# Gated cross-attention and a 64-expert layer on one core: token gathers held by landings instead of progress marks, and the last softmax sums moved ahead of the last values

## The reference

```python
x = x + tanh(g_xattn) * xattn(layernorm(x), ctx_512)     # x: (2, 256, 256)
x = x + tanh(g_ffn) * ffn(layernorm(x))

def xattn(q, latent_kv):                  # 16 heads of width 16, causal
    qp = q @ Wq.T
    k, v = split(latent_kv @ Wkv_expand.T)      # latent_kv: (2, 512, 64)
    attn = softmax(where(causal, qp_h @ k_h.T / 4, min))
    return (attn @ v) @ Wout.T

def ffn(x):                               # 512 tokens, 64 experts, the best 8 of each token
    topw, topi = top_k(softmax(x @ router_weight.T), 8); topw = topw / sum(topw)
    # each expert takes the first 128 of its tokens, in the tokens' order
    h = silu(xe @ gate) * (xe @ up)       # 256 -> 96 for each half
    ye = h @ down                         # 96 -> 256
    return sum over a token's 8 experts of topw * ye
```

## Time and profile before

| | |
|---|---|
| median of 3 runs | 226.35 us (223.43 to 227.15) |
| the profiled execution's own time | 225.09 us |
| its span, first to last instruction | 223.3 us |
| TensorE matmul busy | 209.1 us, 94% |
| VectorE busy | 140.0 us, 63% |
| ScalarE busy | 110.4 us, 49% |
| GpSimd busy | 105.5 us, 47% |
| granted TensorE clock | 1.00 of full speed, in all 40 slices |

### The profile page before, as it was taken

The page is one execution under the profiler, slowest core; times in us unless marked ns, Lnnn a source line. Parts: engine busy times, 40 slices in busy tenths (PEclk is TensorE's granted clock), DMA queues, the critical chain, the costliest instruction groups (busy, mean ns, idle before and its releaser), DMA issues.

```text
span 223.3 us, 5260 instructions
## 1 busy us (share of the span) xinstructions
PE 209.1 (94%) x1676; PEld 166.2 (74%) x1676; DVE 140.0 (63%) x443; ACT 110.4 (49%) x350; POOL 105.5 (47%) x145
## 2 busy tenths in 40 slices
PE   7889999999999779899999899998989999999983
PEld 3556767776557247688998798888879888999973
DVE  6366354476498976637666665656666656348765
ACT  2525445434634926555555564645665555444431
POOL 7301222222262457555655556575555754756630
PEclk9999999999999999999999999999999999999999
DMA  5699999999011234787898898988755655223222
GB/s 153 191 301 282 305 283 250 246 251 236 23 59 23 68 103 128 208 222 217 237 288 245 255 250 276 246 252 276 212 141 160 173 157 157 73 70 83 84 70 94
DMA packets 37725, 41.03 MB, mean 184 GB/s; under 512 B 3874, under 2 KB 35044, under 8 KB 37700
## 3 DMA queue, kind: packets, MB, share of 16 engines
q1 hardware_dynamic: 32932, 27.21, 43.8%
q0 software_dynamic: 4048, 12.98, 22.0%
q10 hardware_dynamic: 720, 0.52, 0.8%
HBM read 32.97 MB, written 7.74 MB: 182 GB/s over the span
## 4 chain that ended last, share of the span: by engine, by line
PE 69%; DVE 8%; DMA 8%; issue 6%; ACT 3%; POOL 2%; another core or an unknown queue 2%; ACTq 0%; DVEq 0%; POOLq 0%
PE bank L789 13%; PE scores L807 10%; PE bank L779 8%; PE scores L779 6%; PE scores L769 6%; PE bank L574 5%; PE bank L589 4%; PE bank L813 4%; DMA gate_w<-xn_dram,slot_token 3%; PE scores L555 3%; DMA gate_w<-in_ctx_dram 3%; PE bank L518 2%; PE bank L537 2%; DMA xe<-xn_dram,slot_token 2%
## 5 line engine op out<-in xcount | busy, mean ns | idle before, releaser
L497 POOL DMA_INDIRECT gate_w<-xn_dram,slot_token x56 | 57.7, 1031 | 40.4 <-issue 15.0
L789 PE MATMUL bank<-y_high,scatter 128*128 128x256 f32 x156 | 45.0, 315 | 0.1
L789 PE MATMUL bank<-y_low,scatter 128*128 128x256 f32 x156 | 39.7, 281 | 0.0
L1280 DVE TENSOR_SCALAR scatter<-tokens,slot_token 128x256 fp32r<-128x256 f32 (+1 forms) x64 | 24.9, 390 | 22.9 <-PE bank L789 19.2
L807 PE MATMUL scores<-down_all,work 96*128 96x256 f32 x128 | 38.2, 380 | 0.7 <-DVE y_low L1293 0.7
L1003 ACT ACTIVATE gate_w<-scores,gate_w 128x256 f32<-128x256 f32 x42 | 20.0, 475 | 27.9 <-PE scores L807 16.3
L428 POOL TENSOR_SCALAR_AFFINE_SELECT gate_w<-gate_w 128x256 f32<-128x256 f32 x32 | 12.2, 406 | 44.2 <-ACT gate_w L904 44.2
L789 PEld LDWEIGHTS bank<-y_high,scatter 128*128 128x128 f32 x156 | 29.5, 189 | 2.3 <-issue 0.5
L789 PEld LDWEIGHTS bank<-y_low,scatter 128*128 128x128 f32 x156 | 29.8, 191 | 0.1
L779 PE MATMUL scores<-gate_w,work 128*128 128x192 f32 x128 | 26.5, 329 | 0.9 <-ACT work L978 0.9
L779 PE MATMUL bank<-gate_w,work 128*128 128x192 f32 x128 | 26.5, 330 | 0.4 <-ACT work L978 0.4
(11 more groups left out here) (193 smaller groups left out, 338.1 us busy)
## 6 DMA issues: line engine op xcount, KB each, us to landing
gate_w<-_L_ffn_gate_up_proj_dram SPq DMA_DIRECT2D x8, 768.0 KB, 10.8
down_all<-in_L_ffn_down_proj_dram SPq DMA_DIRECT2D x16, 384.0 KB, 9.2
gate_w<-_L_ffn_gate_up_proj_dram SPq DMA_DIRECT2D x32, 192.0 KB
ye_dram<-gate_w SPq DMA_DIRECT2D x42, 128.0 KB
gate_w<-xn_dram,slot_token POOLq DMA_INDIRECT x56
ye_dram<-xe SPq DMA_DIRECT2D x5, 128.0 KB
x_sb<-in_x_dram SPq DMA_DIRECT2D x2, 256.0 KB, 4.7
ye_dram<-xn SPq DMA_DIRECT2D x3, 128.0 KB
```

Source lines behind the costliest of these rows:

```text
L497: pool.indirect_dma_start(out=rows, out_offset=None, in_=xn2_dram, in_offset=bass.IndirectOffsetOnAxis(ap=slot_token[:, e:e + 1], axis=0), ...
L789: last = nc.tensor.matmul(bank[6 + t // 2][:, t % 2 * H:t % 2 * H + H], scatter[e % 2][:, t * P:t * P + P], (y_high, y_low)[part][e % 2][: ...
L1280: v.tensor_scalar(scatter[e % 2][:, 0:wide], tokens[:, 0:wide], slot_token[:, e:e + 1], None, ALU.is_equal).then_inc(scatter_done, 1)
```

## The change

1. `pace_tokens` is gone, with the constant `PACED_FROM`, and with it the waits on `xeT_done` for 3 <= e < 10. Instead gather e waits until gather e - 2 has landed; for 10 <= e < 40 until gather e - 3 has landed. The wait for the landing of e-8 goes, since the new one implies it. `free_after` and the lists stay. The new wait begins at e = 2.
2. The sums of the last pair of attention rounds go to `bank[2]` instead of `bank[6]`. In the last round all sums are issued ahead of the values, with a signal of their own, `last_sums`; ScalarE's `invert_sums` waits for it instead of `pv_done`. `normalise_values` waits for `pv_done` too, in all four pairs.

```diff
+        def on_the_way(e):
+            return 3 if SINGLES + 3 <= e < RESERVED + XE_SEMS else 2
...
+        def sums_of(pair):
+            return bank[6][:, S:2 * S] if pair < QUADS // 2 - 1 else bank[2][:, 0:S]
...
-            def pace_tokens(i):
-                n, mark = PACED_FROM - 4 + i // 7 * 6, i % 7
-                if mark == 0:
-                    pool.wait_ge(gu_mm, n + 1)
-                elif mark == 1:
-                    pool.wait_ge(xeT_done, n + 3)
...
-                if e >= XE_SEMS:
-                    pool.wait_ge(xe_in[e % XE_SEMS], 16 * (e // XE_SEMS))
                 if free_after:
                     pool.wait_ge(gu_mm, free_after)
-                if 3 <= e < PACED_FROM:
-                    pool.wait_ge(xeT_done, e - 2)
-                elif e >= PACED_FROM:
-                    pace_tokens(e - PACED_FROM)
+                landed = e - on_the_way(e)
+                if landed >= 0:
+                    pool.wait_ge(xe_in[landed % XE_SEMS], 16 * (landed // XE_SEMS) + 16)
                 pool.indirect_dma_start(
...
             def attend(i, kt):
...
+                if i < QUADS - 1:
+                    weigh_values(i, kt)
+                    last = sum_up(i, kt)
+                    if kt:
+                        last.then_inc(pv_done, 1)
+                elif kt == 0:
+                    sum_up(i, 0)
+                else:
+                    sum_up(i, 1).then_inc(last_sums, 1)
+                    weigh_values(i, 0)
+                    weigh_values(i, 1).then_inc(pv_done, 1)
...
             def invert_sums(pair):
-                act.wait_ge(pv_done, 2 * pair + 2)
+                if pair < QUADS // 2 - 1:
+                    act.wait_ge(pv_done, 2 * pair + 2)
+                else:
+                    act.wait_ge(last_sums, 1)
...
-                nc.scalar.activation(rden, bank[6][:, S:2 * S], ACT.Ln).then_inc(den_logged, 1)
+                nc.scalar.activation(rden, sums_of(pair), ACT.Ln).then_inc(den_logged, 1)
...
             def normalise_values(pair):
                 dve.wait_ge(rden_done, pair + 1)
+                dve.wait_ge(pv_done, 2 * pair + 2)
```

More of the change, by code:

```diff
@@ L58 @@
 RANK_CHUNKS = 2
-PACED_FROM = 10
 LATE_FROM = 2
@@ L238, in flamingo_moe @@
         scored_again, exped, causal, pv_done = (sem(n) for n in ("scored_again", "exped", "causal", "pv_done"))
-        router_centred = sem("router_centred")
+        router_centred, last_sums = sem("router_centred"), sem("last_sums")
         den_logged, rden_done = sem("den_logged"), sem("rden_done")
@@ L454, in _ @@
             pool.wait_ge(xn2_stored, 16 * (QT + len(ROUTES)))
-            def pace_tokens(i):
-                n, mark = PACED_FROM - 4 + i // 7 * 6, i % 7
-                if mark == 0:
-                    pool.wait_ge(gu_mm, n + 1)
-                elif mark == 1:
-                    pool.wait_ge(xeT_done, n + 3)
-                elif mark == 2:
-                    pool.wait_ge(xe_turned, n + 4)
-                elif mark == 3:
-                    pool.wait_ge(y_mm, n + 1)
-                elif mark == 4:
-                    pool.wait_ge(hid_done, n + 4)
-                elif mark == 5:
-                    pool.wait_ge(silu_done, n + 5)
-                else:
-                    pool.wait_ge(hid_turned, n + 5)
             def pace_rows(c):
@@ L578, in score_again, with weigh_values, sum_up @@
                             last.then_inc(scored_again, 1)
+            def weigh_values(i, kt):
+                b, g, y = quad_of(i)
+                for j in range(4):
+                    last = nc.tensor.matmul(bank[6][HP * j:HP * j + HP, kt * P:S], v_sb[:, QT * b + kt, 8 * g + 2 * j + y, :],
+                                            probT[i % 2][:, j, kt * 2 * P:2 * P + kt * P],
+                                            start=(y == 0 and kt == 0), stop=(y == 1 and kt == 1), skip_group_check=True)
+                return last
+            def sum_up(i, kt):
+                y = quad_of(i)[2]
+                for j in range(4):
+                    last = nc.tensor.matmul(sums_of(i // 2)[HP * j:HP * j + HP, kt * P:S], ones_of[:, y, :],
+                                            probT[i % 2][:, j, kt * 2 * P:2 * P + kt * P],
+                                            start=(i // 2 == QUADS // 2 - 1 and y == 0 and kt == 0),
+                                            stop=(y == 1 and kt == 1), skip_group_check=True)
+                return last
             def attend(i, kt):
-                b, g, y = quad_of(i)
+                y = quad_of(i)[2]
                 pe.wait_ge(causal, 4 * i + 3 + kt)
@@ L585, in attend @@
                     pe.wait_ge(attT_done, i // 2)
-                for den in (0, 1):
-                    for j in range(4):
-                        weights = ones_of[:, y, :] if den else v_sb[:, QT * b + kt, 8 * g + 2 * j + y, :]
-                        last = nc.tensor.matmul(bank[6][HP * j:HP * j + HP, den * S + kt * P:den * S + S], weights,
-                                                probT[i % 2][:, j, kt * 2 * P:2 * P + kt * P],
-                                                start=(y == 0 and kt == 0 and den == 0),
-                                                stop=(y == 1 and kt == 1), skip_group_check=True)
-                if kt:
-                    last.then_inc(pv_done, 1)
+                if i < QUADS - 1:
[9 more added lines that the diff above has]
+                    weigh_values(i, 1).then_inc(pv_done, 1)
             def project(n):
```

## The result

The changed kernel takes 236.5 us (median of 4 runs, 234.85 to 236.88), the kernel before 226.74 us: the ratio is 1.051, 95% interval 1.041 to 1.061. It is slower by some 10 us, where 228.0 us was forecast, in a range up to 232.0. The profiled execution took 236.88 us, with a span of 235.1.

The account below looks back on a forecast made before the run. TensorE, busy 94% of the span, was taken as the bound, with early gathers on the chain that ended last. 225.09 + 2.9 (early gathers) + 0 + 0 + 0 = 228.0 us, own range 226.3 to 230, overall range 224.6 to 232.0.

Parts of the forecast that it names:

- Early gathers: Gathers 2 to 9, two on their way: expert 9's rows come 2.9 us later, carried to the end, +2.9 us.
- Sums edit: Last attention round: reciprocals up to 1.2 us sooner, but VectorE's own chain sets the normalisation's start; gain 0.
- middle gathers: Gathers 10 to 39, three on their way: one in 1.75 us against TensorE's 1.88; cost nothing.
- Gathers 40 to 63 and the row gathers: End of GpSimd's queue: gather 63 at 195.2 us, first rows there 201.3, wanted 204.2; cushion 2.9 us, cost nothing.
- row gathers late: GpSimd's queue from gather 40: mean latency above 3.55 us makes first rows late, stopping VectorE and TensorE; 232 us, chance 0.15.
- Starved in the middle: Gathers 10 to 39: latency above 4.9 us slows each expert, about 4 us more; 232 us, chance 0.08.
- Less contention: ScalarE's stops and TensorE's waits for its copy: thinner gather flow gives back 2.3 us; 222.8 us, chance 0.10.
- Keep up: Token gathers: with fewer on their way each may land faster, so nothing is lost; 225.1 us, chance 0.20.

Follow-up runs that it names:

- after: The changed kernel as it is, against the kernel before: 1.051 in the first pair, 1.049 and 1.063 when run again.
- the two kernels above: Kernel before with only gathers 40 to 63 waiting for landings, 1.046, and kernel before with only the row gathers held until 60 gate and up products, 1.041.
- both mended: Changed kernel with gathers 2 to 9 on their old marks and three on their way from 40 on; 1.001 of the kernel before.
- calm set: First, third or fifth set of follow-up runs: the kernel before took 219 us and no profile shows a "remote" wait.
- uneasy sets: Second and fourth sets of follow-up runs: the kernel before took 227 and 224 us and every profile has several "remote" waits.
- late gathers alone: Kernel before with only gathers 40 to 63 waiting for landings, two on their way, no edit of the sums; 1.046 of the kernel before.
- rows late: Kernel before with only the first row gather held until 60 gate and up products, the others without marks; 1.066 (second set), 1.071, 1.041.

## Why the prediction was wrong

**Early gathers: right.** The step said +2.9 us by 0.76 us from release to start and latencies of 14.06 us in sum. By the rows above, the four starts came 0.71, 0.87, 0.71 and 0.73 us behind the landings (3.0 in sum, 3.04 forecast), and the latencies were 3.3, 3.6, 3.75 and 4.0 (14.6). That makes +3.5; alone, in time, 3.3 us. Its place, mechanism and price were right. The estimate of 2.4 us for such a gather, by the Trainium skill's DMA: Bandwidth & Descriptors, "Anatomy of one DMA", does not agree with these rows: all four took longer.

**Sums edit and middle gathers: right,** both 0, 1.003 and 1.000 measured. VectorE's chain hides the one, three on the way is fast enough for the other.

**Gathers 40 to 63 and the row gathers: the step that failed.** It is the sentence "a cushion of 2.9 us ... Cost nothing". The gathers came later and were wanted sooner than the step had it, and the lateness cost more. In four terms:

1. Gather 40 was put at 148.5 us and went at 151.01. It waited for the landing of gather 38, which was issued at 145.25. With 0.70 us from landing to start, 38's latency was about 5.1 us, where 4.5 was taken throughout.
2. From there 23 x 2.03 = 46.7 us was forecast with a latency of 3.3, and it took 49.1 us, 2.14 each, that is 2 x 2.14 - 0.70 = 3.6 us of latency. I had taken a value near the upper bounds of two early gathers (3.24 and 3.36) though the very same held 3.7 and 4.06. Together with the first term, gather 63 went 5.0 us after its forecast of 195.2.
3. The need was put at 201.30 + 2.9 = 204.2; VectorE was ready at 198.51 + 0.48 = 199.0. The 201.30 came from an execution that had lost about 5 us in stops of ScalarE (4.2 us) and VectorE (2.3 us), which needn't come back. In after's profile TensorE was ahead of it by 1.6 us at expert 59 in spite of the early loss. The prediction read these stops only as a possible gain; they were also part of the cushion of a transfer. The stop is what remains: the first row had landed at 204.28, 5.28 us behind 199.0.
4. The price. The rival "row gathers late" had this place and mechanism, and a threshold of 3.55 us of latency that 3.6 exceeds, but it priced 4 us of lateness at 4 us and got 0.15. Two things make it dearer. One is the half clock behind the stop (2.7 and 3.0 us in the two kernels above). The other is a misreading: "two every three steps" is the wrong way round, `2 * c // 3` asks for three rows in two steps. Two steps are 4.74 us, so a row is wanted every 1.58 us on average and, with the last ones bunched, all in 18.4 us (both mended), while issuing them takes 15 x 1.31 = 19.7 us. There is no later slack to give the time back, and the end hangs on the first row gather.

The two measured profiles differ by 10.4 us when expert 63's rows are loaded (219.05 against 208.68). By the times of these weight loads it is +3.5 up to expert 9, -5.1 from there to 59 (the stops of before that are not in after), +7.5 from 60 to 62 (the stop and the half clock) and +4.5 from 62 to 63 (the "remote" stop at 216 us); another 1.4 us come behind it. So the 1.051 is in part luck: a gain of 5.1 us that belongs to one execution of before, and a loss of 4.5 us of a kind that no calm set shows, nearly cancel.

Whether the early and the late part add up is open: alone they are 1.015 and 1.046, together 1.049 to 1.063, and only in uneasy sets. The changed kernel itself was not run in a calm set. Its three profiles all have the "remote" stop between experts 62 and 63, where the step takes 6.9 to 8.0 us instead of 2.37; what brings it there is open too.

**The other rivals.** "Starved in the middle" did not occur. "Less contention" is refuted as a gain of the change: "remote" stops are absent from every profile of the calm sets, marks or landings, and present in the uneasy ones whatever paces the gathers. "Keep up" fell with the latencies above 3.2 us.

## What to carry to other kernels

In a queue that issues in order, the price of a slower pace is set by the last thing in the queue: follow the lag to the item behind which the end waits, here 16 row gathers with a pace of their own, and not just to the items that are paced. Take a cushion as the difference of two times that each have an error: work it out with the shortest time to the need (without stops that may not return) and the longest latency seen, and where it is gone, add the clock to the stop. Then hold the pace at which the later items are wanted against the pace at which they can be issued, all the way to the last: only the difference gives lateness back. A transfer that only the end needs should not be waited for ahead of work that feeds the bounding engine; but moving the wait back helps only if the transfers' own pace leaves room.

## What the runs showed of the hardware

- TensorE stops of 4.1 to 5.8 us between busy stretches were each followed by a half-speed stretch: granted clock 0.50 from 204 to 210 us with the late gathers alone, after 4.92 us of stop, and full clock again from 210; 0.50 from 219 to 224 us in after, behind the stop of 4.09 us.
- The time from a gather's landing to the start of the next indirect DMA that waited for it on GpSimd was 0.70 to 0.87 us in every place read; back to back, such DMAs start about 1.31 us apart at best.
- Unnamed stops of up to 6 us on ScalarE, VectorE and GpSimd come in some sets of runs in all kernels and in others (all on chip 0) not at all; the kernel before took 224 to 227 us in the ones and 219 in the others. Their places differ by kernel, but the longest recur in the same kernel on different chips: in all three profiles of after in the same step. Packets of instruction fetches don't settle it: in rows late (second set) one lies at 223 us, inside the stop from 221.5 to 227.3, in after none lies inside the stop from 212 to 216.4, and late gathers alone has one at 213 without such a stop. Their cause is open.
- Issuing gathers 3 to 6 up to 2.3 us sooner, and gather 9 1.0 us sooner, landed the rows of expert 9 only 0.13 us sooner (96.12 against 96.25 us in the same set).
